# Third attention stage: six slots per pair instead of four, squares on ScalarE, last sum on VectorE

## What is computed

```
def _L2_attn_ref(x, W_embed, b_embed, W_out, b_out):
    ...
    def head(W, b):
        e = jnp.einsum('bmc,hc->bmh', x, W) + b
        q, k, v = jnp.split(e, 3, axis=1)
        attn = jax.nn.softmax(jnp.einsum('bmd,bnd->bmn', q, k) * SCALE, axis=-1)
        return jnp.einsum('bmn,bnd->bmd', attn, v)
    outs = jax.vmap(head)(W_embed, b_embed)
    qkv = jnp.concatenate([outs[i] for i in range(outs.shape[0])], axis=1)
    out = jnp.einsum('bmd,cd->bmc', qkv, W_out) + b_out
    return out + x
...
h = h + _L2_attn_ref(_layernorm(h, axis=-1), L2_attn_W_embed, L2_attn_b_embed, L2_attn_W_out, L2_attn_b_out)
```

## Time and profile before

| what | us |
|---|---|
| median of three runs (4523.86 to 4526.0) | 4524.99 |
| the profiled execution, its own time | 4523.71 |
| its span in the trace | 4521.8 |
| the stage, from its weights being ready to the first DMA of the store of pair 29 | 2184.1 to 2471.7 |
| from the first DMA of the store of pair 0 to that of pair 27 | 2209.53 to 2456.24 |

### The profile page before, as it was taken

How to read it: one execution, slowest core, us unless ns; L and a number is a source line. 1 busy time by engine, 2 the same in 40 slices (tenths; PEclk the granted TensorE clock), 3 DMA queues, 4 the chain that set the end, 5 groups by cost and what they waited for, 6 DMA issues and landing times.

```text
span 4521.8 us, 111329 instructions
## 1 busy us (share of the span) xinstructions
PE 3874.9 (86%) x31697; PEld 2646.6 (59%) x31697; DVE 2827.4 (63%) x9288; ACT 2307.5 (51%) x5837; POOL 2091.1 (46%) x2436
## 2 busy tenths in 40 slices
PE   7488847677999889999766777999999999899999
PEld 7355523465666656666665444666666666555555
DVE  2577735555788744444344676888888888455554
ACT  5455524211444434444222335888888888555555
POOL 0144337664566422222576563555555555443333
PEclk9999966697999989999655677999999999999999
DMA  1111123222111233333111220000000000233332
GB/s 52 37 31 31 28 50 98 73 56 47 32 37 37 56 82 74 81 80 74 35 42 42 54 51 23 15 12 11 11 11 14 12 11 9 59 76 75 77 78 59
DMA packets 483330, 207.55 MB, mean 46 GB/s; under 512 B 452850, under 2 KB 473326, under 8 KB 482930
## 3 DMA queue, kind: packets, MB, share of 16 engines
q1 hardware_dynamic: 483058, 204.73, 19.9%
HBM read 158.75 MB, written 45.91 MB: 45 GB/s over the span
## 4 chain that ended last, share of the span: by engine, by line
PE 48%; issue 19%; POOL 15%; DVE 9%; SPq 5%; ACT 2%; DMA 1%; POOLq 1%; DVEq 0%; ACTq 0%
POOL att_P L3554 8%; PE sw_pH L4156 5%; PE moe_pH L2714 4%; PE sw_pY L4143 4%; PE moe_pY L2737 4%; DVE att_M L1175 3%; PE att_pS L980 3%; PE moe_pH L2718 2%; PE moe_pH L2724 2%; PE ret_pR L1832 2%; POOL att_norm_rstd L673 1%; PE att_pS L2207 1%; SPq L2881 1%; PE att_pO L1042 1%; SPq L2869 1%
## 5 line engine op out<-in xcount | busy, mean ns | idle before, releaser
L3554 POOL TENSOR_TENSOR att_P<-att_P,att_rden 125x498 f32<-125x498 f32 x512 | 521.0, 1018 | 511.7 <-DVE att_rden L3849 511.2
L3742 ACT ACTIVATE att_P<-att_Z,att_nb 125x249 f32<-125x249 f32 x1024 | 501.5, 494 | 50.8 <-issue 27.9
L2779 DVE TENSOR_TENSOR moe_hT<-moe_silu,moe_pH 128x498 f32<-128x498 f32 x384 | 258.8, 674 | 306.8 <-ACT moe_silu L2763 306.8
L4204 ACT ACTIVATE sw_hT<-sw_pH,sw_b 128x498 f32<-128x498 f32 x512 | 318.3, 673 | 219.4 <-PE sw_pH L4156 219.4
L3663 PEld LDWEIGHTS att_pP<-att_ident,att_P 124*125 124x125 f32 (+1 forms) x2048 | 263.0, 187 | 234.8 <-issue 234.6
L3663 PE MATMUL att_pP<-att_ident,att_P 124*125 124x124 f32 (+1 forms) x2048 | 350.4, 293 | 49.7 <-issue 28.2
L3861 DVE CUSTOM_DVE_ANT_0 att_Z<-att_pS,att_mask 125x249 f32<-125x249 f32 x1024 | 365.8, 412 | 29.5 <-PE att_pS L3651 27.5
L2763 ACT ACTIVATE moe_silu<-moe_pH 128x498 f32<-128x498 f32 x384 | 225.3, 587 | 262.2 <-PE moe_pH L2718 176.3
L3749 ACT ACTIVATE att_PTr<-att_pP 125x498 f32<-125x498 f32 x512 | 296.7, 579 | 76.6 <-PE att_pP L3663 70.3
L2690 POOL TENSOR_TENSOR moe_xe<-moe_share,moe_x 128x1992 f32<-128x1992 f32 x32 | 130.1, 4065 | 427.9 <-DMA moe_share<-mixing 347.6
L4063 POOL TENSOR_TENSOR sw_acc<-sw_acc,sw_Z 128x249 f32<-128x249 f32 x224 | 154.5, 690 | 363.4 <-DVE sw_Z L4283 362.7
(11 more groups left out here) (463 smaller groups left out, 9815.2 us busy)
## 6 DMA issues: line engine op xcount, KB each, us to landing
moe_share<-mixing SPq DMA_DIRECT2D x64, 498.0 KB, 6.1
sw_share<-mixing SPq DMA_DIRECT2D x64, 498.0 KB, 5.6
ffn_W<-in_ffn_pairs SPq DMA_DIRECT2D x64, 192.0 KB, 2.4
att_F<-h_stream SPq DMA_DIRECT2D x192, 62.5 KB
att_X<-h_stream SPq DMA_DIRECT2D x192, 62.5 KB
h_stream<-att_H SPq DMA_DIRECT2D x64, 62.5 KB
ffn_F<-h_stream SPq DMA_DIRECT2D x64, 62.5 KB
ret_F<-h_stream SPq DMA_DIRECT2D x64, 62.5 KB
```

Of the source, the lines that this page charges most:

```text
L3554: g.tensor_tensor(own, own, bc(rden[:, j % 2, c, :], T), ALU.mult).then_inc(*scaled.one())
L3742: ins = a.activation(P[:, r, c, t, :], Z[:, r, c, t, :], ACT.Exp, scale=-1.0, bias=nb[:, r, c, t:t + 1], accum_out=den[:, r, c, t:t + 1])
L4204: a.activation(hT[:, k % 4, :, :], pH[:, place, :, 0:T], ACT.Relu, bias=b1[:, k:k + 1]).then_inc(*hid_ready.one())
```

## The change

STEPS goes from 4 to 5 and the parts from four to six: `pre`, `even`, `turn_in`, `proj`, `soft`, `ends`. The sums of a pair stand in step 4 of its slot, the centring in step 3 and the squares in step 4 of the next slot, `spread`, power, scale and transposition in the slot after (`turn_in`), A and V in the fourth (`proj`), scores and exponentials in the fifth (`soft`), and the rest in the sixth (`ends`). The squares go from GpSimd (`norm.square`, L647) to ScalarE (`norm.square_scalar`, L652). The last sum of a pair, H1 = tmp + base, goes from GpSimd to VectorE, right behind tmp. `WAVES` and `ROUNDS` only tell a counter how many copies of the code there are. SP's list, and with it the lead of its loads, is not touched.

```
-    STEPS, WAVES = 4, 6
+    STEPS, WAVES, ROUNDS = 5, 8, 6
...
         def _(g):
-            def pre(n, u, step):
-                if step == 0:
+            def even(n, u, step):
+                if step == 3:
                     g.wait_ge(*xn_ready.before(n))
                     norm.center(g, n, g4(F[:, u, :, :, :]))
-                if step == 1:
-                    norm.square(g, n)
-                if step == 3:
+            def turn_in(n, u, step):
+                if step == 2:
                     norm.power(g, n)
...
-                if step == 2:
+                if step == 1:
                     g.wait_ge(*biased.after(n))
...
-            def ends(n, u, step):
-                if step == 3:
-                    g.wait_ge(*o_ready.after(n))
-                    g.wait_ge(*base_ready.after(n))
-                    g.wait_ge(*stored.lagging(n, u))
-                    st.held(g)
-                    g.tensor_tensor(g4(H1[:, u, :, :, :]), tmp[:, :, :], g4(base[:, u, :, :, :]),
-                                    ALU.add).then_inc(*h_ready.one())
-            waves(g, (pre, nothing, soft, ends), STEPS)
+            waves(g, (nothing, even, turn_in, nothing, soft, nothing), STEPS)
...
         def _(pe):
...
-            def proj(n, u, step):
-                if step == 0:
+            def turn_in(n, u, step):
+                if step == 3:
                     pe.wait_ge(*xn_ready.after(n))
                     pe.wait_ge(*xT_ready.before(n))
...
-                if step == 1:
+
+            def proj(n, u, step):
+                if step == 2:
                     pe.wait_ge(*xT_ready.after(n))
                     pe.wait_ge(*a_ready.before(n))
...
-                if step == 3:
                     pe.wait_ge(*v_ready.before(n))
...
             def soft(n, u, step):
-                if step == 0:
+                if step == 1:
                     pe.wait_ge(*a_ready.after(n))
...
-                if step == 2:
+                if step == 3:
                     pe.wait_ge(*pt_ready.after(n))
...
-            waves(pe, (nothing, proj, soft, ends), STEPS)
+            waves(pe, (nothing, nothing, turn_in, proj, soft, ends), STEPS)
...
         def _(a):
...
-            def proj(n, u, step):
-                if step == 0:
+            def even(n, u, step):
+                if step == 4:
+                    norm.square_scalar(a, n)
+
+            def turn_in(n, u, step):
+                if step == 4:
                     a.wait_ge(*xT_done.after(n))
                     a.activation(xT[:, u, :], pX[:, 0:T], ACT.Copy).then_inc(*xT_ready.one())
-                if step == 3:
+
+            def proj(n, u, step):
+                if step == 4:
                     a.wait_ge(*v_done.after(n))
...
-            waves(a, (nothing, proj, soft, nothing), STEPS)
+            waves(a, (nothing, even, turn_in, proj, soft, nothing), STEPS)
...
         def _(v):
             def pre(n, u, step):
-                if step == 0:
-                    v.wait_ge(*loaded.after(n, u))
-                    norm.sums(v, n, g4(F[:, u, :, :, :]))
+                if step == 4:
+                    v.wait_ge(*loaded.after(n, u))
+                    v.wait_ge(*norm.centered.before(n))
+                    norm.sums(v, n, g4(F[:, u, :, :, :]))
+            def turn_in(n, u, step):
+                if step == 0:
+                    norm.spread(v, n, 1e-5)
...
             def proj(n, u, step):
-                if step == 1:
...
                 if step == 2:
-                    norm.spread(v, n, 1e-5)
...
                     v.wait_ge(*a_done.after(n))
...
             def soft(n, u, step):
-                if step == 0:
+                if step == 1:
                     v.wait_ge(*s_done.after(n))
...
                     v.wait_ge(*o_done.after(n))
                     v.tensor_tensor(tmp[:, :, :], pO[:, 0:GR * C].rearrange("p (g c) -> p g c", g=GR),
                                     bc(rden[:, :], C), ALU.mult).then_inc(*o_ready.one())
+                    v.wait_ge(*o_ready.after(n))
+                    v.wait_ge(*base_ready.after(n))
+                    v.wait_ge(*stored.lagging(n, u))
+                    st.held(v)
+                    v.tensor_tensor(g4(H1[:, u, :, :, :]), tmp[:, :, :], g4(base[:, u, :, :, :]),
+                                    ALU.add).then_inc(*h_ready.one())
-            waves(v, (pre, proj, soft, ends), STEPS)
+            waves(v, (pre, nothing, turn_in, proj, soft, ends), STEPS)
```

More of the change, by code:

```diff
@@ L2843, in stage_attention2 @@
         weights = st.event("weights")
-        loaded = st.transfers("loaded", bodies=WAVES)
-        kept = st.transfers("kept", bodies=WAVES)
-        stored = st.transfers("stored", bodies=WAVES)
+        loaded = st.transfers("loaded", bodies=ROUNDS)
+        kept = st.transfers("kept", bodies=ROUNDS)
+        stored = st.transfers("stored", bodies=ROUNDS)
         names = """xn_ready xT_done xT_ready a_done a_ready v_done v_ready s_done max_ready exp_ready pt_done pt_ready
```

## The result

| | median us | runs |
|---|---|---|
| the kernel before, beside it on the same chip | 4524.42 | 4514.93 to 4526.0 |
| the changed kernel | 4625.93 | 4619.64 to 4632.53 |
| ratio, with its 95% interval | 1.0231 | 1.0217 to 1.0245 |

The change makes the kernel 101.5 us slower. 4622 was forecast, with 4600 to 4650 as the range. The profiled execution took 4619.64, with a span of 4617.9, 96.1 above the span of before.

A forecast was written before the change was run, and what follows sets the result against it. SP's DMA issues, 9.14 us a pair, were taken as the bound, replaced after the change by a ring of 12.91 us over 27 pairs. 4523.71 + 101.9 - 1.2 - 3.0 = 4621.4, predicted as 4622, range 4600 to 4650.

The forecast's parts named there:

- The lead of the loads: SP issues load F of pair s behind store s-5, whose last sum VectorE makes just before row sums needing F(s).
- The ring: Last sum, store, load F, landing, row sums to next last sum: closed once a pair, 27 times, 12.91 us each.
- The terms of a turn: Seven steps from one H1's end to the next: 0.24 + 5.95 + 1.09 + 0.76 + 0.86 + 2.87 + 1.14 = 12.91 us.
- step 7: End of a turn on VectorE: tmp 0.55, 0.04 to the next, then H1 taken as 0.55; 1.14 us in all.
- The 6.27 among the bounds: Upper bound in us for store's first DMA to end of load F, using the 3.05 store that waited; 5.95 was put.
- Fill and drain: Stage's start and end: first store 1.2 us earlier; last slots at TensorE's 6.11 us each, 3.0 us less.
- The signs: Stores 12.9 us apart, SP waiting 3.8 for H1, row sums 7.3 for load F, PE about 48%, POOL below 40%.
- Squares to ScalarE: Moving squares takes 0.824 us a pair off POOL, adds some 0.5 to ACT; effect on time 0.
- Rival (a): Same ring, dearer: POOL's centring overlaps H1 and holds it up to 0.83 us a pair, +22, 4644; chance 0.10.
- Rows 8: Profile rows cited against a POOL hold: VectorE with both operands in SBUF takes 425 ns, with one in PSUM 424.
- (b): No change: the lead of the loads suffices, SP goes on at 9.14 us a pair, 4519 to 4525; chance 0.04.
- (c): Faster: POOL sets SP's pace through a full queue, 1.81 us less on POOL gives -49 us, 4475; chance 0.03.

The follow-up runs named there:

- e1: The changed kernel with load F issued one pair earlier in SP's list (n+5 instead of n+4 ahead of store n): 4516.12 us, 0.9982 of before.
- e4: The kernel before, four slots kept, with only squares moved to ScalarE and the last sum to VectorE: 4520.07 us, 0.9993 of before.
- e5: The kernel before with F, X, H1 and base laid out by batch and third, 6 DMA issues a pair instead of 18: 4511.90 us, 0.9976.
- e3: The kernel before with only loads F issued one pair later (n+3 ahead of store n): 4621.15 us, 1.0210 of before.
- e7: The changed kernel with load F one pair earlier and 6 DMA issues a pair: 4451.94 us, 0.9841 of before.
- e9: The kernel before with 6 DMA issues a pair and only the last sum moved to VectorE, four slots: 4456.76 us, 0.9844 of before.
- e8: As e7, with the squares back on GpSimd behind the centring: 4456.86 us, 0.9852 of before.

## Why the prediction was right, point by point

- **What bounds the kernel now.** SP's issues, as read from the chain and from waits that were not there. e1 and e4, which take work from POOL and leave SP its 18 issues, stay at 9.07 and 9.14 a pair; e5, which takes issues from SP and no work from any engine, drops below. What the trace of before could not show, and the text did not say, is that the next bound lay 0.4 us under this one.
- **The lead of the loads.** The ring was read from the two lists, not from a row. The 27 waits of VectorE for load F and the 30 of SP for the last sum show it, e1 opens it, e3 closes it elsewhere.
- **The terms of a turn**, from the turns of 2398 to 2424: H1 to store 0.26 and 0.25 (0.24); store's first DMA to end of load F 6.06 and 5.79 (5.95); landing 0.99 and 1.18 (1.09); row sums and `spread` 1.83 in one half of the loop, with 0.31 of "issue" in it, and 1.32 in the other, 1.58 in the mean (0.76 + 0.86 = 1.62); PTr to tmp 2.87 (2.87). The term that was mis-sized is step 7: from tmp's start to the end of H1 1.29 and 1.36 where 1.14 was put. H1 itself takes 0.554, as taken; but VectorE stands 0.19 to 0.25 between its own tmp and H1, where I had taken 0.04 from a row sum and its scaling. H1 has two more waits in front of it, so how much of this is due to tmp is not shown. In the mean of the 27 turns step 7 is 1.32, the landing 1.15, row sums and `spread` 1.55, and the other terms are within 0.02 of what was put. So 13.08 exceeds 12.91 by 0.17 a turn, 4.5 us in 27 turns: 353.13 - 246.71 = +106.4 in place of +101.9. That row sums and `spread` came so close is partly luck: the 0.86 of before held a scaling (L660) of 0.36, which takes 0.17 now, and the gap of 0.31 in every other turn gives most of it back. The 6.27 among the bounds is in no row: with the store of 3.05, store and load F took 6.07.
- **Fill and drain.** From load F of pair 4 to the first store 10.32 us, where before had 10.87: -0.6 in place of -1.2. PTr to tmp took 3.40 in this first turn, as TensorE was still at A and V. From the store of pair 27 to that of pair 29 13.47, where before had 15.48: -2.0 in place of -3.0, as the two slots of TensorE took 7.04 and 6.57 from pO to pO and not 6.11 each. The 6.11 was a slot in the old order of TensorE's groups. In the new order the same products take longer: 6.56 from pO to pO in e7, where TensorE does not stand, against 6.1 in e9, which keeps the old order (6.71 a pair less 0.6 of waiting ahead of the transposes). Why is not shown. The stage in all: 106.42 - 0.55 - 2.01 = +103.9, where +97.7 was forecast.
- **The rest of the program.** The span grew by 96.1 only. Load F of pair 4 began 7.15 us earlier than in the trace of before, so the stages ahead of the edited one, whose code is the same, were that much faster in this execution; over 1090 to 1590 us the granted clock was 0.95 in place of 0.94. Behind the store of pair 29 the changed one is 0.6 us shorter. The medians of the four timed runs lie 101.5 apart, between the two; how they divide is in no trace. That the total came within 4 us of the forecast is thus partly luck, as the stage cost 6 us more than was summed.
- **The signs.** Stores 13.08 apart, SP waiting 30 times for H1 (115.1 us, 3.8 each), 27 waits for load F of 7.3 each and POOL at 39% came as named. TensorE's share did not: 53% where 48 was put, as a product of the new order is recorded as busy for 0.160 us (53.45 over 335) and one of the old order for 0.142 (67.36 over 473).
- **Squares to ScalarE.** 0.535 us on ACT (0.5 was estimated), and nothing that can be told in the time: e4, and e8 against e7.
- **Rival (a)**, the port held at H1, did not come: H1 takes 0.554 on average, as long as tmp, and GpSimd's centring is over when it starts (2410.82 and 2411.13, and 2397.62 and 2397.76 in the other half of the loop), while the next bias sum waits for it. It was near: 0.14 us in that half. Rows 8 were weak evidence against the hold, as the trace of before has it at other lines (last section). The fixed cost of about 2.0 us that the Trainium skill states ("DMA: Bandwidth & Descriptors", Anatomy of one DMA) for a DMA issued by GpSimd would have given an estimated 18 us more here; landings of 0.99 to 1.28 on SP's queue disagree with it as the rows of before did. **Rivals (b) and (c)** fall with the 30 waits of SP, (c) also with e4, where 1.8 us a pair less on POOL give nothing.

## What to carry to other kernels

Before a pipeline is made deeper, count the lead of its loads against the new depth: if the load for pair s is issued behind a store that waits for a result which the reader of that load makes just ahead of it, the depth buys a ring of store, load and landing once a pair. A ring is found by following one queue's order and one engine's order, and its length is a sum of rows most of which the old trace already has. Before work is moved from an engine, look whether anything waits for that engine last; here a queue that counts as busy nowhere hid a second ring only 0.4 us shorter, and both edits together, fewer issues and the moved sum, gave what neither gave alone (0.2% in e5, and nothing in e4, where the squares moved along, against 1.6% in e9).

## What the runs showed of the hardware

A hold such as rival (a) spoke of does occur, in other places, and the trace of before had it already. There VectorE's scaling of the row sums, six numbers a row, takes 0.17 us when it starts ahead of GpSimd's scaling (ten times from 2250 to 2460, as at 2345.15 in the earlier trace rows). When GpSimd's starts with it or up to 0.14 us ahead (six times), it ends with GpSimd's, after 0.72 to 0.84 us; a few hundredths decide, as it takes 0.17 at 2372.58 with GpSimd's start at 2372.60, and 0.83 at 2409.14 with that at 2409.11 (VectorE's and GpSimd's timelines):

```profile
2445.70 0.84 DVE L637 TENSOR_SCALAR att_norm_sum<-att_norm_sum 83x6 f32<-83x6 f32 x1
...
2445.70 0.83 POOL L679 TENSOR_TENSOR att_xn<-att_norm_centered,att_norm_rstd 83x384 f32<-83x384 f32 x1 [0.17 <-POOL att_norm_rstd L673]
```

In e9, where the last sum on VectorE, with both operands in SBUF, and GpSimd's scaling do meet, it is GpSimd, the later, that is longer: 1.043 us on average against 0.825 in the changed kernel (e9's timelines of the two engines).

```profile
2303.90 0.56 DVE L3138 TENSOR_TENSOR att_H<-att_tmp,att_base 83x384 f32<-83x384 f32 x1 [0.25 <-DVE att_tmp L3132]
...
2304.07 1.07 POOL L2939 TENSOR_TENSOR att_xn<-att_norm_centered,att_norm_rstd 83x384 f32<-83x384 f32 x1 [0.17 <-POOL att_norm_rstd L673]
```

The Trainium skill ("SBUF — State Buffer", Who interferes with whom) says that whichever instruction starts first has the shared port and the other waits; which one is longer in these rows agrees with it. GpSimd's delay in e9 is shorter than the overlap, though: 0.25 where the two overlap by 0.39, and 0.19 where they overlap by 0.33. In e9 the scaling also writes through a permuted view; e7 does that too and its scaling takes 0.82, so the view is not the cause. The scaling lies on e9's chain, but what the hold costs e9 in time was not tried.
